# Second graph's pass over the edges: two PSUM banks for the placings, each issued two quarters ahead of its selections

## The reference

```
hh     = (x @ W).reshape(n, 8, 32)
s_src, s_dst = einsum(hh, a_src), einsum(hh, a_dst)          # 8 scores a node
scores = leaky_relu(s_src[src] + s_dst[dst], 0.2)            # 8 an edge
e      = exp(scores - segment_max(scores, dst)[dst])
alpha  = e / segment_sum(e, dst)[dst]
out    = segment_sum(hh[src] * alpha, dst)
out    = elu(layer_norm(out + x))
```

## Time and profile before

| | us |
|---|---|
| median of three runs (5453.67 to 5479.73) | 5473.58 |
| span of the profiled execution, first to last instruction | 5404.7 |
| median less that span | 68.9 |
| TensorE matmuls busy in the span | 3933.5 (73%) |
| VectorE busy | 3064.0 (57%) |
| GpSimd busy | 2464.9 (46%) |
| ScalarE busy | 1859.8 (34%) |

### The profile page before, as it was taken

The page is one execution under the profiler, slowest core; times in us unless marked ns, Lnnn a source line. Parts: engine busy times, 40 slices in busy tenths (PEclk is TensorE's granted clock), DMA queues, the critical chain, the costliest instruction groups (busy, mean ns, idle before and its releaser), DMA issues. The chain is left out here.

```text
span 5404.7 us, 69347 instructions
## 1 busy us (share of the span) xinstructions
PE 3933.5 (73%) x16281; PEld 2847.1 (53%) x16282; DVE 3064.0 (57%) x7623; ACT 1859.8 (34%) x5073; POOL 2464.9 (46%) x2442
## 2 busy tenths in 40 slices
PE   6867777777777659967853666666666338999999
PEld 4545555555555448856732444444444226777776
DVE  3278887878888766662154666666667773111111
ACT  1333333333333312311222444444444322333332
POOL 2256665656666450001166666666663422333332
PEclk8988988888888879977986788777887559999999
DMA  2555555555555232211173333333331451111111
GB/s 80 186 146 149 154 151 148 151 140 153 147 148 151 83 118 84 91 55 40 52 252 89 95 96 96 94 95 94 93 96 47 127 194 20 32 32 31 31 31 27
DMA packets 316127, 553.64 MB, mean 102 GB/s; under 512 B 63431, under 2 KB 213783, under 8 KB 315857
## 3 DMA queue, kind: packets, MB, share of 16 engines
q0 software_dynamic: 137120, 388.63, 27.4%
q1 hardware_dynamic: 178736, 161.98, 9.8%
HBM read 459.75 MB, written 90.62 MB: 102 GB/s over the span
## 5 line engine op out<-in xcount | busy, mean ns | idle before, releaser
L427 POOL DMA_INDIRECT attend_ring<-kv_rows,all_step_src x880 | 860.1, 977 | 624.5 <-PE attend_ps_agg L468 371.3
L931 POOL DMA_INDIRECT edge_ring<-head_rows,all_step_src x880 | 878.7, 999 | 457.1 <-issue 204.2
L967 PE MATMUL edge_ps_agg<-edge_msg,edge_sel 128*128 128x264 f32 x1760 | 676.3, 520 | 188.9 <-issue 57.3
L468 PE MATMUL attend_ps_agg<-attend_msg,attend_sel 128*128 128x264 f32 x1760 | 605.1, 445 | 179.7 <-DVE graph_qa L785 122.9
L967 PEld LDWEIGHTS edge_ps_agg<-edge_msg,edge_sel 128*128 128x128 f32 x1760 | 414.5, 257 | 328.2 <-issue 198.7
L1266 DVE TENSOR_TENSOR graph_acc<-graph_acc,edge_ps_agg 128x264 f32 x880 | 369.9, 420 | 367.2 <-PE edge_ps_agg L967 169.0
L2821 DVE TENSOR_TENSOR moe_gl<-moe_ps_h,moe_act 128x341 f32<-128x341 f32 x210 | 107.8, 514 | 776.8 <-PE moe_ps_h L2739 776.8
L452 PE MATMUL attend_ps_q<-graph_qa,attend_sel_t 128*128 x1760 | 527.7, 429 | 27.4 <-ACT attend_sel_t L581 17.8
L785 DVE SCALAR_TENSOR_TENSOR graph_qa<-graph_qa,all_step_same,attend_ps_agg 128x264 f32 x880 | 421.1, 479 | 170.1 <-remote 121.0
L468 PEld LDWEIGHTS attend_ps_agg<-attend_msg,attend_sel 128*128 128x128 f32 x1760 | 329.3, 208 | 347.2 <-issue 148.6
L2739 PE MATMUL moe_ps_h<-experts_w,moe_xt 128*128 x1680 | 501.7, 451 | 0.6 <-ACT moe_xt L2770 0.6
(11 more groups left out here) (424 smaller groups left out, 6587.9 us busy)
## 6 DMA issues: line engine op xcount, KB each, us to landing
attend_ring<-kv_rows,all_step_src POOLq DMA_INDIRECT x880
edge_ring<-head_rows,all_step_src POOLq DMA_INDIRECT x880
kv_rows<-qkv_kv SPq DMA_DIRECT2D x25, 512.0 KB, 2.9
experts_w<-in_w_t SPq DMA_DIRECT2D x16, 682.0 KB
attend_mask<-run_starts SPq DMA_DIRECT2D x440, 8.1 KB
edge_mask<-run_starts SPq DMA_DIRECT2D x440, 8.1 KB
head_rows<-hds_hh SPq DMA_DIRECT2D x25, 264.0 KB
qkv_x<-in_x SPq DMA_DIRECT2D x25, 256.0 KB, 3.3
```

The costliest lines, as they stand in the source:

```text
L427: nc.gpsimd.indirect_dma_start(ring[:, step % RING1, :], None, g.kv_rows, bass.IndirectOffsetOnAxis(g.step_src[:, step:step + 1], 0)).then ...
L468: nc.tensor.matmul(ps_agg[i % SUM_BANKS][:, 0:AGG], sel[:, q % 2, u % QU, :], msg[:, q % 2, u % QU, :], start=True, stop=True).then_inc(s_ ...
L931: nc.gpsimd.indirect_dma_start(ring[:, n % slots, u, :], None, g.head_rows, bass.IndirectOffsetOnAxis(g.step_src[:, step:step + 1], 0)).th ...
L967: nc.tensor.matmul(ps_agg[i % BANKS][:, 0:AGG], sel[:, q % 2, u % QU, :], msg[:, q % 2, u % QU, :], start=True, stop=True).then_inc(s_agg, 1)
```

## The change

`ps_gt` becomes two tiles of one bank each, used in turn. With the three banks of the sums and the three other PSUM tiles this makes eight tiles instead of seven. Each placing is issued one quarter earlier in TensorE's order: behind `at_node` of quarter k stands the placing of quarter k+2 instead of k+1, and it waits for the same count of `s_rt`. Two placings stand ahead of the first `at_node`. ScalarE's order is the same; its L1069 reads the tile of its quarter.

```diff
-        ps_gt = m.ps("ps_gt", [P, QU, P])
+        ps_gt = [m.ps(f"ps_gt{i}", [P, QU, P]) for i in range(2)]
...
-                if k >= 1:
-                    pe.wait_ge(s_rt, k)
-                nc.tensor.matmul(ps_gt[:].rearrange("p u e -> p (u e)"), g.lane_feat[:],
+                if k >= 2:
+                    pe.wait_ge(s_rt, k - 1)
+                nc.tensor.matmul(ps_gt[k % 2][:].rearrange("p u e -> p (u e)"), g.lane_feat[:],
...
+            place_t(0, 0)
+            place_t(0, 1)
             for half in range(2):
                 blocks = blocks_of(0, half)
                 for q in (2 * half, 2 * half + 1):
-                    place_t(0, q)
                     at_node(0, q, blocks)
-            place_t(1, 0)
+                    place_t(*divmod(q + 2, quarters))
...
                     at_node(c, 0, ahead)
-                    place_t(c, 1)
+                    place_t(c, 2)
...
                     at_node(c, 1, ahead)
-                    place_t(c, 2)
+                    place_t(c, 3)
...
                     at_node(c, 2, blocks)
-                    place_t(c, 3)
+                if after:
+                    place_t(c + 1, 0)
...
                     at_node(c, 3, blocks)
                 if after:
-                    place_t(c + 1, 0)
+                    place_t(c + 1, 1)
...
-                nc.scalar.activation(sel_t[:, q % 2], ps_gt[:], ACT.Relu, bias=1.0, scale=-1.0).then_inc(s_rt, 1)
+                nc.scalar.activation(sel_t[:, q % 2], ps_gt[k % 2][:], ACT.Relu, bias=1.0, scale=-1.0).then_inc(s_rt, 1)
```

## The result

The changed kernel takes 5455.71 us (median of 20 runs) where the kernel before, on the same chip, takes 5469.55 (20 runs, 5453.67 to 5496.9). The ratio is 0.9972, with a 95% interval of 0.9958 to 0.9985, so it is 8 to 23 us faster: a real gain, and by the bound of 0.5% no change. Two of the 20 runs of the changed kernel took 9798 and 14283 us, in a slow state, and are left out of the ratio; the median of the other 18 is 5454.9. The trace of before has a span of 5404.7 us, 49 us under the quickest of the 20 timed runs of that kernel, so it is no sample of them. The two traces can't be subtracted as a whole: the pass over the edges in the first graph attention, which nobody touched, takes 1573.6 us in that of before and 1612.3 in the other, 38.7 apart (first to last gather).

The account below looks back on a forecast made before the run. A ring of waits, with GpSimd's gathers setting the beat and two holds a chunk, was taken to bound the pass. Span 5404.7 - 3.7 (1.2 + 2.5, all at the start) plus 68.9 around it gave 5469.9 us; own range 5455 to 5482, overall 5420 to 5502.

Parts of the forecast that it names:

- (a): ScalarE's selection 1 runs before the chunk's first hold (TensorE's results seen late): price 0, bounds 0 and 0.60 us a chunk.
- (b): Selection 3 runs inside the second hold, so sum 12 can start earlier; slack, price 0, bounds 0 and 0.74 us a chunk.
- (c): GpSimd's two pauses a chunk end with the holds, and between them its gathers keep 1.26 us spacing: price 0.
- E: Rival: GpSimd's pauses go and a chunk comes down to 20.2 us, 190 us less, 5284; chance 0.05.
- (d): Start of the pass: second placing 1.2 us earlier, copy of the weights gains 2.5 us; 3.7 us less in all.
- B: Rival, faster: the 0.74 us is on the path in 40 chunks where TensorE waited for the selection, 30 us, 5444; chance 0.22.
- C: Rival, slower: the two-pause pattern breaks, GpSimd pauses a third time in more chunks, 31 us, 5505; chance 0.18.
- D: Rival: placings are held as long where they now stand, ScalarE's waits and the time stay, 5473; chance 0.05.

Follow-up runs that it names:

- The square of runs: Second bank alone, placings two quarters ahead in the first two chunks only, later only, or both (the change): 0.9997, 0.9983, 0.9971, 0.9983 of the kernel before.

## Why the prediction was right, and where not

The forecast was 5469.9 us in 5420 to 5502 and "no change" as the likeliest; 5455.71 is in the range, and the ratio says 0.28% less than before. The sum, -3.7 us, lies outside the measured -8 to -23, so being in a range of 82 us is no proof of the sum. Of the 14.2 us between forecast and result, 4.0 are the median of before, 5473.58 from three runs and 5469.55 from 20; the other 10.2 are gain that the sum doesn't have. The span was forecast at 5401.0 and came to 5439.2; that the time was nearer is because the 68.9 us around the span, which belong to a trace out of line with its timed runs, were carried over (median less span is 16.5 us for the changed kernel).

**(a) and (b), selections 1 and 3 earlier, priced 0.** What was foreseen of one chunk came to the hundredth: the selections stand behind the denominators, their waits fell by 258.6 of 381.1 us, sum 12 starts 0.58 us after the hold's end for 1.32 before (3522.50 - 3521.92, 3486.61 - 3485.29), the 0.74 us of the text, and the chain from there to the first sum of the next chunk is 7.67 us in both traces (3521.92 to 3529.59; the earlier trace rows: 3485.29 to 3492.96), so they are slack in this chunk. To the hundredth is luck: the text let sum 12 start 0.43 us after the hold's end, which would have been 0.89 earlier and not 0.74. One sign was wrong: TensorE's wait ahead of that first sum fell from 1.74 to 1.53 and didn't grow; of the slack 0.48 went into the six sums behind the hold, 3.13 us for 2.65. The failed step is the price over the pass. I took the chunk of the usual kind, found 0, and multiplied; the other chunks, with their extra pauses, were 15 of 50 in that trace (13 by the count of pauses above) and left as they were. The square of runs gives -9.3 us plus or minus 5.9 for this part, -0.19 a chunk, within the bounds of 0 to 0.74 and not at the end that I chose.

**(c), the pauses.** They stay, two in 39 of 50 chunks. E fell.

**(d), the start.** Second placing: from the first gather to the one that waits for it 26.3 us for 27.6 (2857.23 - 2830.89; 2823.55 - 2795.9), 1.3 earlier for a predicted 1.2. The copy of the weights: 93.9 us after the first gather for 98.3, so 4.4 earlier for a predicted 3.7; the exponential itself 11.7 earlier, beyond the 9.6 (1.2 + 8.4) that was to be the upper bound, and as foreseen the turning back fell into a hold and took most of that away again. (Of the 15 us that the prediction gives (d) for its own range, its terms account for these 9.6.) The gather of chunk 4 came 4.4 earlier. Six further traces give 3.2 us on the chip of the square (97.6 and 98.7 us for 101.6 and 101.1 at one quarter) and 2.6 on the one without holds. The Trainium skill, "Perfetto Trace Analysis", has a matmul's end as an estimate; here the placing's time of arrival, and not its end in the trace, was what counted, and it was 22.7 us behind that end at its worst (2883.21 - 2860.54).

**B** priced the 0.74 us in 40 chunks at 30 us: too much by three, and for another reason. **C** asked the right question, whether two pauses or three, and gave it the wrong sign: it feared that the change would break the pattern; two quarters of lead held it, and it is the kernel with one that shows it broken in two of three traces. (Its example, the chunk from 4073.20 to 4097.29, has by the count above the pauses 1.37, 1.66 and one of 1.60 at 4090.89 that was passed over; the 2.49 belongs to the chunk before. At 24.09 us it is no longer than a chunk of two.) The prediction had even said that the pattern "is no property of the program", and drew nothing from it. **D** is refuted by the waits of ScalarE. **E**'s argument that the holds might be TensorE's own order, for which the section "Who interferes with whom" of "SBUF — State Buffer" in the Trainium skill was named, found no support: ScalarE's waits fell by two thirds, and the holds stayed, at GpSimd's pauses.

Open: what makes TensorE's results late on some chips. That in the fifty chunks holds end soon after GpSimd stops is shown, and that at the start of the pass they don't; which of the two brings about the other is not, since GpSimd's pauses are themselves waits for late sums. That holds would be gone without gathers was not tried on a chip that has them. That the gain of 9.3 us comes by chunks of three pauses becoming rarer is what six traces point to; why a late selection should make one is argued from one chunk.

## What to carry to other kernels

When the chunks of a loop come in kinds, count the kinds before a price is multiplied: a wait that is slack in the usual chunk may decide how many are usual. One trace can't give that count, least of all the quickest of its kernel. And before a wait is loosened to let a queue run ahead, ask who is stopped while that queue runs: here the changed kernel with one semaphore exchanged for an earlier one took 98 us longer than the kernel before.

## What the runs showed of the hardware

- The same kernel took 5421 to 5470 us in three sets of runs on at least two chips and 5031 to 5034 on another (on two occasions), at granted clocks over the pass of 0.78 and 0.77. In this pass, which holds 153 to 185 us of the difference, the chips part in when other engines see TensorE's results: 0.62 us after a placing's start there; here 4.8 us in the chunk shown, up to 6.4 in the fifty chunks and 23 at the start.
- On the chips with holds, 465 of 487 holds in the fifty chunks ended while GpSimd stood still, some 1.4 to 1.9 us after its last gather. At the start of the pass one ended 5.7 to 8.2 us after it.
- An indirect gather occupies GpSimd nearly as long for 64 rows (1.22 us from start to start) as for 128 (1.26).
- On the chip without holds a chunk took 20.9 us with its gathers and 17.4 us without, and the granted clock in the pass was 0.77 and 0.88.
